# Dropping the value projection in the first stage: the sum over keys is taken over the normalised rows

## The chip, the cores and the metric

The kernel runs on one core of a Trainium2 chip. The metric is the device time of one execution in microseconds (us); lower is better. TensorE is written PE (its weight loads PEld), VectorE DVE, ScalarE ACT, GpSimd POOL, and the queue that issues most DMAs SP. "L672" is line 672 of the kernel before.

## The reference

Four layers follow each other on 16 x 256 tokens of width 128, each as `x = x + layer(layernorm(x))`: a linear attention with a small feed-forward network, a softmax attention with a mixture of experts, a second attention without softmax, and the softmax attention with the experts again. The change lies in the first layer only, whose attention is:

```python
Q = (x @ Wq + bq).reshape(N, L, H, Dh)       # N=16, L=256, H=16, Dh=8
K = (x @ Wk + bk).reshape(N, L, H, Dh)
V = (x @ Wv + bv).reshape(N, L, H, Dh)
Q = jax.nn.elu(Q) + 1.0
K = jax.nn.elu(K) + 1.0
KV = jnp.einsum('nshd,nshm->nhmd', K, V)
Ksum = K.sum(axis=1)
Z = 1.0 / (jnp.einsum('nlhd,nhd->nlh', Q, Ksum) + EPS_ATTN)
out = jnp.einsum('nlhd,nhmd,nlh->nlhm', Q, KV, Z)
```

## The kernel before

The first stage works on 16 pairs of 128-row tiles (one pair is one sequence of 256 tokens). It is a software pipeline written out by hand: on every engine `body(i, ...)` is emitted for i = 0, 1, 2, ..., and inside body i each block `if has(k)` does its step for pair p = i - k. An engine does its instructions in exactly this order, and where it waits for a semaphore (`wait_ge`, `after`), all that is queued behind waits too. Different engines use different k for the same pair, since each counts its own bodies.

TensorE's body i consists of, in this order (all matrix products are fp32; one such product shows as two matmul records):

- L577: the query product of pair i-1, 256 columns, into QM
- L589: transposes of z1 (second norm), pair i-7; L596: transposes of the attention rows, pair i-3; L606: attention product, pair i-2
- L619: second product of the feed-forward network, pair i-9
- L629: transposes of z0 (the normalised rows), pair i
- L636, L663: first product of the feed-forward network in halves, pairs i-8 and i-7; L647: output projection, pair i-4
- L656: the sum over keys of pair i-1: k_r (the keys after elu + 1) against v_r (the values with a column of ones), two products of 129 columns into KS
- L672: keys and values of pair i, two products of 256 columns into the bank KV

So the first bodies lack most steps: L647 comes in from i = 4, L663 and L589 from i = 7, L636 from i = 8, L619 from i = 9. In bodies 0 to 3 `spin` (L155) issues products of ones that nobody reads: three ahead of L629, one ahead of L672 and one ahead of L606. Body 5 also makes a weight product (L485), after L577.

ScalarE's body i: a relu (L690), z0 of pair i (L697, two instructions), exp of the keys of pair i-1 (L706), the copy of its values (L707), zt1 (L712), att_t (L717), exp of the queries (L722), a relu (L727), tmp (L735), the copy zt of the transposed z0 of pair i (L741, which adds the constant HAT), z1 (L749), and in bodies 4 and 5 a DMA issue (L564), in body 5 also a weight copy (L510).

VectorE makes k_r = max(min(exp, 1), rows) at L846 behind the statistics of a later pair (L537), and masks the sums from KS at L814 and L827. In its body 2 it also makes the small weight folds. GpSimd makes rstd and shift (L913, L915) for the three norms of an iteration in one go.

All weights of the stage carry a constant HAT trick: zt = z + HAT, and the bias row, scaled by ROW = 1/(128 HAT), is added to every row of the weights, so that the product brings the bias with it.

Of the kernel before, what the change touches and what calls it, by code (L numbers as in the profile page):

```python
# [84 lines left out]
def build(nc, A, out):  # L85

    ctx = ExitStack()
    with ctx:
# [41 lines left out]

        wa_qkv = sb("wa_qkv", [P, 3 * D])
        wa_o = sb("wa_o", [P, D])
# [36 lines left out]
        q_t = sb("q_t", [P, 3, 2 * P])  # L169
        v_r = sb("v_r", [P, 3, 2, P + 2])  # L170
        att_t = sb("att_t", [P, 3, 2 * P])
# [224 lines left out]
        hat_kept = sem("hat_kept")  # L396
        tokens_made = sem("tokens_made")
        k_cleared, p_cleared = sem("k_cleared"), sem("p_cleared")
        guarded = sem("guarded")

        @on("vector")
        def _(dve):
            nc.vector.memset(v_r[:, :, :, P:P + 1], 1.0).then_inc(rows_made, 1)
            dve.wait_ge(w_q_in, 16 * len(loads_q))

            nc.vector.tensor_scalar_add(row_a[0:1, 0:2 * D], row_a[0:1, 0:2 * D], 1.0).then_inc(rows_made, 1)

        def folds(dve):

# [12 lines left out]
            nc.vector.tensor_scalar_mul(b_low[:, :], b_low[:, :], 1.0 - 16 * B).then_inc(fold_step, 1)  # L422
            dve.wait_ge(fold_step, 4)
            nc.vector.tensor_scalar(token[:, :], token_f[:, :], b_low[:, 0:1], None, ALU.add).then_inc(tokens_made, 1)

# [3 lines left out]
        def hat(width, lhsT, rhs, bias, dst, **kw):  # L429
# [3 lines left out]

        hats_a = [hat(3 * D, centre[:, :], wa_raw[:, :], row_a[:, :], wa_qkv[:, :]),
                  hat(F, fold_a[:, :], wa1_raw[:, :], row_a2[:, :], wa1[:, :])]
# [98 lines left out]
        def bn(sources, slot, at, done):  # L534
# [5 lines left out]
        a_s = {n: sem("a_" + n) for n in (  # L540
            "n0", "n1", "n2", "step", "rstd", "shift", "z0", "z1", "z2", "turned", "turned1", "zt", "zt1", "kv_q", "read", "phi",
            "sums", "masked", "att", "inv", "att_r", "att_t", "wo", "xz", "r1", "hid", "relu", "w2", "y1", "r2", "xres", "xo")}
        a_stored = [sem(f"a_stored{n}") for n in range(3)]
# [24 lines left out]
        def _(pe):  # L568
# [3 lines left out]
            def body(i, s, has, lap):  # L572
# [36 lines left out]
                if has(9):  # L609
# [6 lines left out]
                    for t in range(2):  # L616
                        cut = slice(t * P, (t + 1) * P)
                        for m in range(FC):
                            last = nc.tensor.matmul(W2B[:, cut], hid[:, p % 2, m, cut], wa2[:, m, :], start=(m == 0),  # L619
                                                    stop=(m == FC - 1))  # L620
                    last.then_inc(g["w2"], 1)
                if has(0):
                    if i < 4:
# [25 lines left out]
                if has(1):  # L649
                    p = i - 1  # L650
                    pe.wait_ge(g["read"], first_of_two(p))
                    pe.wait_ge(g["phi"], first_of_two(p))
                    after(pe, g["masked"], p)
                    after(pe, g["r2"], i - 8)
                    for t in range(2):
                        last = nc.tensor.matmul(KS, k_r[:, p % 3, t, :], v_r[:, p % 3, t, 0:P + 1], start=(t == 0), stop=(t == 1))  # L656
                    last.then_inc(g["sums"], 1)
                if has(7):
# [7 lines left out]
                if has(0):  # L666
                    if i < 4:
                        spin(pe, bank[4], 1)
                    pe.wait_ge(g["zt"], i + 1)
                    after(pe, g["phi"], first_of_two(i - 1))  # L670
                    for t in range(2):
                        last = nc.tensor.matmul(KV[:, t * 256:(t + 1) * 256], zt[:, i % 3, 0, t * P:(t + 1) * P],  # L672
                                                wa_qkv[:, D:3 * D], start=True, stop=True)
                    last.then_inc(g["kv_q"], 1)
# [7 lines left out]
        def _(act):  # L682
            g = a_s

            def body(i, s, has, lap):
# [6 lines left out]
                if has(0):  # L692
                    act.wait_ge(g["shift"], i + 1)
                    after(act, g["turned"], i - 2)
                    after(act, g["xz"], i - 2)
                    for t in range(2):
# [3 lines left out]
                if has(1):  # L700
                    p = i - 1
                    act.wait_ge(g["kv_q"], first_of_two(p))
                    after(act, g["phi"], first_of_two(p - 3))
                    after(act, g["sums"], p - 2)
                    rows = KV[:, :].rearrange("p (t n) -> p t n", t=2)
                    nc.scalar.activation(exp_k[:, p % 3, :, :], rows[:, :, 0:P], ACT.Exp, bias=minus1[:, 0:1])  # L706
                    nc.scalar.activation(v_r[:, p % 3, :, 0:P], rows[:, :, P:2 * P], ACT.Copy).then_inc(g["read"], 1)  # L707
                if has(7):
# [29 lines left out]
                if has(0):  # L738
                    act.wait_ge(g["turned"], i + 1)
                    after(act, g["kv_q"], second_of_two(i - 3))  # L740
                    nc.scalar.activation(zt[:, i % 3, 0, :], TT[:, 0:256], ACT.Copy, bias=HAT).then_inc(g["zt"], 1)  # L741
                if has(6):
# [21 lines left out]
        def _(dve):  # L764
# [9 lines left out]
            def body(i, s, has, lap):  # L774
# [67 lines left out]
                if has(3):  # L842
                    p = i - 3
                    dve.wait_ge(g["read"], first_of_two(p))
                    rows = KV[:, :].rearrange("p (t n) -> p t n", t=2)
                    nc.vector.scalar_tensor_tensor(out=k_r[:, p % 3, :, :], in0=exp_k[:, p % 3, :, :], scalar=1.0,  # L846
                                                   in1=rows[:, :, 0:P], op0=ALU.min, op1=ALU.max).then_inc(g["phi"], 1)
                if has(7):
# [28 lines left out]
        def _(pool):  # L877
# [6 lines left out]
            def body(i, s, has, lap):  # L884
# [13 lines left out]
                if has(0) or has(7) or has(12):  # L898
# [15 lines left out]
                    pool.wait_ge(g["rstd"], i + 1)  # L914
                    nc.gpsimd.tensor_tensor(shift[:, c, w], nmean[:, c, w], rstd[:, c, w], ALU.mult).then_inc(g["shift"], 1)  # L915
                if has(12):
# [187 lines left out]
        def attention_block(n, src_dram, stored_before):  # L1104
# [217 lines left out]
            def _(dve):  # L1322
# [148 lines left out]
                else:  # L1471
                    dve.wait_ge(tokens_made, 1)
                nc.vector.memset(hot[:, 2, 1, :], 0.0).then_inc(cleared, 1)
# [230 lines left out]
        def block_b():  # L1704

            b_s = {k: sem("b_" + k) for k in (
                "stats0", "agg", "step", "rstd", "shift", "z", "turned", "zt", "gram", "gram_kept", "xw", "xw_kept", "fac", "fac_kept",
                "bo", "m", "m_kept",
                "out", "x3")}
# [119 lines left out]
            def _(dve):  # L1829
# [27 lines left out]
                dve.wait_ge(w_o_in, 16 * len(loads_o))  # L1857
                nc.vector.tensor_scalar_mul(bo[:, :], bo[:, :], ROW).then_inc(g["bo"], 1)
                dve.wait_ge(g["bo"], 1)
                pipeline(dve, PAIRS, DEPTH, 3, body, FIRST)  # L1860
# [84 lines left out]
```

## Time and profile before

| | before |
|---|---|
| timed runs | 684.54 us median of 3 (683.92 to 684.79) |
| span of the profiled execution | 684.5 us, 19055 instructions; no other time was recorded for it |
| TensorE busy (matmuls) | 637.8 us, 93% |
| TensorE weight loads | 545.5 us, 80% |
| VectorE | 483.9 us, 71% |
| ScalarE | 380.5 us, 56% |
| GpSimd | 398.7 us, 58% |
| the first stage | from the start to about 140 us |

Busy shares are averages over stages with different limits, so they only say where to look. For a stage one reads the waits of its engines and the chain of work that ended last. A record of a matmul is longer than the time it holds the array (records overlap, and their ends include the way through the array); the chain shows the time that each step really takes from the one before.

### The profile page before, as it was taken

The page shows a single profiled execution, that of the slowest core. Times are in us where ns is not written, and L with a number is a line of the kernel's source. Part 1 is how long each engine was busy: PE and PEld are TensorE (multiplying, and loading weights), DVE is VectorE, ACT ScalarE, POOL GpSimd, SP SyncE. Part 2 cuts the span into 40 slices and gives each one's busy share as a digit, 9 for nine tenths or more (in the row PEclk, how much of TensorE's full clock was granted, in tenths as well). Part 3 has the DMA queues.
Part 4 walks back from the last instruction along what each step waited for, and adds up shares of the span by engine and source line. Part 5 has one row for each costly group of instructions (what it writes and reads, how often), then busy time and mean ns, then how long its engine had stood idle before and what let it go on. Part 6 is the DMA issues. An engine that isn't in the chain of part 4 may idle for free.

```text
span 684.5 us, 19055 instructions
## 1 busy us (share of the span) xinstructions
PE 637.8 (93%) x5450; PEld 545.5 (80%) x5450; DVE 483.9 (71%) x2160; ACT 380.5 (56%) x974; POOL 398.7 (58%) x714
## 2 busy tenths in 40 slices
PE   8999999968999899999978999999699999999993
PEld 5899999836778679999975788787577877998993
DVE  2586777759999858888851333324899996887884
ACT  2587777648888435555523333330787864555550
POOL 5466668954688654767751121230548877467666
PEclk9999999989999989999999999999999999999997
DMA  4961001161122441232240000001312224332220
GB/s 126 325 234 30 17 25 33 36 203 27 44 74 88 168 134 54 85 85 78 59 133 7 24 17 24 15 23 49 109 31 73 78 92 119 83 85 76 81 69 21
DMA packets 57929, 53.63 MB, mean 78 GB/s; under 512 B 7707, under 2 KB 52164, under 8 KB 57532
## 3 DMA queue, kind: packets, MB, share of 16 engines
q1 hardware_dynamic: 51050, 36.19, 18.6%
q0 software_dynamic: 5568, 12.96, 5.5%
q10 hardware_dynamic: 1234, 3.55, 1.4%
q8 instruction: 37, 0.61, 0.4%
q14 instruction: 40, 0.33, 0.2%
HBM read 31.33 MB, written 19.83 MB: 75 GB/s over the span
## 4 chain that ended last, share of the span: by engine, by line
PE 44%; DVE 29%; issue 9%; POOL 8%; DVEq 4%; ACT 3%; DMA 2%; SPq 0%; POOLq 0%; ACTq 0%
PE wide L1794 4%; PE wide L1767 4%; DVE hid_f L1670 4%; PE wide L619 4%; PE bank L1780 4%; DVE stats L1666 3%; DVEq L1663 3%; POOL sorted_dram L1509 3%; POOL rstd L1495 3%; PE wide L155 2%; DVE late L1692 2%; PE bank L672 2%; PE wide L636 2%; PE wide L663 2%; PE wide L485 2%
## 5 line engine op out<-in xcount | busy, mean ns | idle before, releaser
L1608 PE MATMUL bank<-zt,late 128*128 128x128 f32 x624 | 92.8, 284 | 5.1 <-DVE hid_f L1670 4.7
L1608 PEld LDWEIGHTS bank<-zt,late 128*128 128x128 f32 x624 | 79.8, 191 | 11.9 <-DVE hid_f L1670 10.2
L1509 POOL DMA_INDIRECT sorted_dram<-rows_e,pos x64 | 66.0, 1031 | 26.1 <-issue 15.5
L1551 POOL TENSOR_TENSOR rstd<-var_e,half_neg 128x1 f32<-128x1 f32 x78 | 47.8, 613 | 43.3 <-DVE xout L1687 30.2
L1631 ACT ACTIVATE late<-we 128x512 f32 x80 | 50.5, 631 | 26.8 <-PE bank L1608 20.2
L1619 PE MATMUL wide<-late,hid_f 128*128 128x128 f32 x416 | 55.1, 275 | 1.1 <-DVE tmp L1675 1.1
L1619 PEld LDWEIGHTS wide<-late,hid_f 128*128 128x128 f32 x416 | 50.6, 192 | 1.4 <-issue 1.4
L1746 POOL TENSOR_TENSOR var_m<-mvs,eps 128x2 f32<-128x2 f32 x16 | 3.1, 194 | 79.5 <-DVE mvs L1847 79.5
L1851 DVE COPY late<-wide 128x1024 f32<-128x1024 f32 x16 | 19.6, 1225 | 39.0 <-PE wide L1794 39.0
L1558 POOL DMA_INDIRECT out<-xout,dest x39 | 40.6, 1041 | 10.4 <-issue 10.4
L1558 POOL DMA_INDIRECT x_dram<-xout,dest x39 | 40.5, 1039 | 8.1 <-issue 8.1
L1278 ACT ACTIVATE rows_e<-tmp,shift,rstd 128x128 f32<-128x128 f32 x64 | 28.1, 487 | 30.6 <-POOL shift L1497 30.6
L1638 ACT ACTIVATE zt<-bank 128x128 f32<-128x128 f32 x78 | 21.6, 277 | 41.7 <-PE bank L1598 39.9
L1495 POOL TENSOR_TENSOR rstd<-var_m,half_neg 128x2 f32<-128x2 f32 (+1 forms) x50 | 40.2, 804 | 4.3 <-DVE nmean L1380 0.9
L1492 POOL TENSOR_TENSOR var_m<-mvs,eps 128x2 f32<-128x2 f32 (+1 forms) x40 | 9.1, 228 | 56.6 <-DVE mvs L1442 26.5
L537 DVE BATCH_NORM_STATS2 stats<-xa 128x6 f32<-128x128 f32 (+1 forms) x128 | 29.4, 271 | 15.9 <-DMA xa<-x_dram 10.0
L1295 ACT ACTIVATE z<-xa,shift,rstd 128x128 f32<-128x128 f32 x64 | 28.0, 489 | 21.9 <-POOL shift L1497 21.9
L155 PE MATMUL wide<-ones 128*128 128x256 f32 x120 | 37.0, 447 | 3.2 <-DVE we L504 1.2
L1692 DVE COPY late<-we 128x640 f32 x78 | 38.2, 490 | 1.7 <-issue 1.7
L1670 DVE TENSOR_SCALAR hid_f<-bank 128x256 f32<-128x256 f32 x78 | 33.1, 425 | 6.7 <-issue 1.6
L1641 ACT ACTIVATE hid_f<-bank 128x256 f32<-128x256 f32 x78 | 29.9, 384 | 13.7 <-PE bank L1608 13.7
L1844 DVE TENSOR_TENSOR m_sb<-bank,bo 128x128 f32<-128x128 f32 x16 | 4.7, 292 | 39.2 <-PE bank L1780 39.2
(300 smaller groups left out, 1947.3 us busy)
## 6 DMA issues: line engine op xcount, KB each, us to landing
rows_e<-sorted_dram SPq DMA_DIRECT2D x78, 128.5 KB, 2.1
xa<-x_dram SPq DMA_DIRECT2D x9, 640.0 KB, 6.0
we<-L_ffn_W SPq DMA_DIRECT2D x16, 256.0 KB
x_dram<-xout SPq DMA_DIRECT2D x32, 128.0 KB, 1.8
early<-late SPq DMA_DIRECT2D x128, 32.0 KB
sorted_dram<-L_attn_a_x ACTq DMA_DIRECT2D x2, 1028.0 KB
rows_e<-L_ffn_b SPq DMA_DIRECT2D x1, 1024.0 KB
hid_f<-L_ffn_b ACTq DMA_DIRECT2D x1, 1024.0 KB
```

The lines of the kernel that those rows point to most:

```text
L155: nc.tensor.matmul(to[:, 0:2 * P], ones[:, :], ones2, start=True, stop=True)
L537: last = nc.vector.bn_stats(stats[:, slot, at + n, :], x)
L1495: nc.gpsimd.tensor_tensor(rstd[:, c, w], var_m[:, c, w], half_neg[:, w], ALU.pow).then_inc(g["rstd"], 1)
L1509: nc.gpsimd.indirect_dma_start(sorted_dram[n][:, :], bass.IndirectOffsetOnAxis(ap=pos[:, p % 3, t:t + 1], axis=0), pay[:, p % PAYS, t, :], ...
L1551: nc.gpsimd.tensor_tensor(rstd[:, s % 3, 0:1], var_e[:, s % 3, :], half_neg[:, 0:1], ALU.pow).then_inc(g["rstd"], 1)
L1558: nc.gpsimd.indirect_dma_start(target, bass.IndirectOffsetOnAxis(ap=dest[:, c, :], axis=0), xout[:, c, 0, :], None, bounds_check=T - 1, oo ...
L1608: last = nc.tensor.matmul(to[:, (m % 2) * P:(m % 2 + 1) * P], we_t[:, c1, m * P:(m + 1) * P], zt[:, c1, 0, 0:P], start=True, stop=True)
L1619: nc.tensor.matmul(VB[c2][:, 0:P], hid_e[:, c2, m, :], we_t[:, c2, F + m * P:F + (m + 1) * P], start=(m == 0), stop=False)
L1631: nc.scalar.activation(we_t[:, c, 0:F], we[:, bass.ds(e, 1), 0:F].rearrange("p a n -> p (a n)"), ACT.Copy).then_inc(g["w1"], 1)
L1641: nc.scalar.activation(hid_e[:, c1, 0:2, :], HA_[:, 0:256].rearrange("p (m t) -> p m t", m=2), ACT.Relu).then_inc(g["relu_a"], 1)
L1670: nc.vector.tensor_scalar_max(hid_e[:, c1, 2:4, :], HB_[:, 0:256].rearrange("p (m t) -> p m t", m=2), 0.0).then_inc(g["relu_b"], 1)
L1692: nc.vector.tensor_copy(we_t[:, c, F:], we[:, bass.ds(e, 1), F:].rearrange("p a n -> p (a n)"))\
```

## The change

The value projection goes. L672 makes only the keys (two products of 128 columns), and the sum over keys is taken over z0 itself, kz = z0^T k_r, in a new step on TensorE; ScalarE copies kz from PSUM to SBUF (new instruction), and one product of kz with the value weights (and a column ROW) gives the sums in KS. The values' copy L707 goes. The new step for pair i-1 stands ahead of L629 and, in bodies 0 to 3, ahead of the three spins; the product into KS stays where L656 was and now waits for the copy of kz, which ScalarE does right behind zt of pair i. Since z0 now takes part as rows with HAT in them, GpSimd adds HAT to shift in one more instruction, and zt is copied without it. The semaphore for two small VectorE steps is merged into another.

```diff
-        wa_qkv = sb("wa_qkv", [P, 3 * D])
+        wa_qkv = sb("wa_qkv", [P, 3 * D + 1])
...
-            nc.vector.memset(v_r[:, :, :, P:P + 1], 1.0).then_inc(rows_made, 1)
+            nc.vector.memset(wa_qkv[:, 3 * D:], ROW).then_inc(rows_made, 1)
```

TensorE, behind L619:

```diff
+                if has(1):
+                    p = i - 1
+                    pe.wait_ge(g["phi"], first_of_two(p))
+                    after(pe, g["kz_kept"], p)
+                    for t in range(2):
+                        last = nc.tensor.matmul(KV[:, 256:256 + P], z0[:, p % 3, t, :], k_r[:, p % 3, t, :], start=(t == 0),
+                                                stop=(t == 1))
+                    last.then_inc(g["kz"], 1)
                 if has(0):
                     if i < 4:
                         spin(pe, bank[4], 3)
...
                 if has(1):
                     p = i - 1
-                    pe.wait_ge(g["read"], first_of_two(p))
-                    pe.wait_ge(g["phi"], first_of_two(p))
+                    pe.wait_ge(g["kz_kept"], p + 1)
                     after(pe, g["masked"], p)
                     after(pe, g["r2"], i - 8)
-                    for t in range(2):
-                        last = nc.tensor.matmul(KS, k_r[:, p % 3, t, :], v_r[:, p % 3, t, 0:P + 1], start=(t == 0), stop=(t == 1))
-                    last.then_inc(g["sums"], 1)
+                    nc.tensor.matmul(KS, kz[:, p % 3, :], wa_qkv[:, 2 * D:], start=True, stop=True).then_inc(g["sums"], 1)
...
                     pe.wait_ge(g["zt"], i + 1)
                     after(pe, g["phi"], first_of_two(i - 1))
+                    after(pe, g["kz_kept"], i)
                     for t in range(2):
-                        last = nc.tensor.matmul(KV[:, t * 256:(t + 1) * 256], zt[:, i % 3, 0, t * P:(t + 1) * P],
-                                                wa_qkv[:, D:3 * D], start=True, stop=True)
+                        last = nc.tensor.matmul(KV[:, t * P:(t + 1) * P], zt[:, i % 3, 0, t * P:(t + 1) * P],
+                                                wa_qkv[:, D:2 * D], start=True, stop=True)
```

ScalarE:

```diff
                     act.wait_ge(g["kv_q"], first_of_two(p))
                     after(act, g["phi"], first_of_two(p - 3))
-                    after(act, g["sums"], p - 2)
-                    rows = KV[:, :].rearrange("p (t n) -> p t n", t=2)
-                    nc.scalar.activation(exp_k[:, p % 3, :, :], rows[:, :, 0:P], ACT.Exp, bias=minus1[:, 0:1])
-                    nc.scalar.activation(v_r[:, p % 3, :, 0:P], rows[:, :, P:2 * P], ACT.Copy).then_inc(g["read"], 1)
+                    nc.scalar.activation(exp_k[:, p % 3, :, :], KV[:, 0:256].rearrange("p (t n) -> p t n", t=2), ACT.Exp,
+                                         bias=minus1[:, 0:1]).then_inc(g["read"], 1)
...
-                    nc.scalar.activation(zt[:, i % 3, 0, :], TT[:, 0:256], ACT.Copy, bias=HAT).then_inc(g["zt"], 1)
+                    nc.scalar.activation(zt[:, i % 3, 0, :], TT[:, 0:256], ACT.Copy).then_inc(g["zt"], 1)
+                if has(1):
+                    p = i - 1
+                    act.wait_ge(g["kz"], p + 1)
+                    after(act, g["sums"], p - 2)
+                    nc.scalar.activation(kz[:, p % 3, :], KV[:, 256:256 + P], ACT.Copy).then_inc(g["kz_kept"], 1)
```

VectorE makes the same k_r from KV[:, 0:256] and waits ahead of it for the kz of three pairs before. GpSimd:

```diff
-                    nc.gpsimd.tensor_tensor(shift[:, c, w], nmean[:, c, w], rstd[:, c, w], ALU.mult).then_inc(g["shift"], 1)
+                    made = nc.gpsimd.tensor_tensor(shift[:, c, w], nmean[:, c, w], rstd[:, c, w], ALU.mult)
+                    if has(0):
+                        made.then_inc(g["centred"], 1)
+                        pool.wait_ge(g["centred"], i + 1)
+                        made = nc.gpsimd.tensor_tensor(shift[:, c, 0:2], shift[:, c, 0:2], hats[:, 0, 0:2], ALU.add)
+                    made.then_inc(g["shift"], 1)
```

## Rows read from the trace of the kernel before

**Rows 1.** Waits of PE from 10 to 131 us: who waited for whom, total us, times, longest.
```profile
PE wide L155 <- ACT wa_qkv L510: 0.6, 1, 0.6
```

**Rows 2.** Chain that ended last, two steady iterations: start us, us, engine, line, records.
```profile
61.03 0.45 PE wide L656 x4
...
62.34 0.86 PE bank L672 x4
...
64.57 1.78 PE wide L619 x16
66.35 0.22 PE bank L629 x2
66.57 0.87 PE wide L636 x4
67.44 0.45 PE wide L647 x4
67.88 0.45 PE wide L656 x4
```

**Rows 3.** The same chain in the first bodies and in body 5.
```profile
14.21 0.95 PE bank L672 x4
15.16 0.43 PE bank L577 x2
15.59 1.29 PE wide L155 x6
...
31.93 1.91 PE wide L485 x4
```

**Rows 4.** Timeline of all engines around pair 0: start us, us, engine, line, names.
```profile
15.20 0.47 ACT L706 ACTIVATE late<-bank,minus 128x256 f32<-128x256 f32 x1 [0.46 <-PE bank L672]
...
15.45 0.45 DVE L537 BATCH_NORM_STATS2 stats<-xa 128x6 f32<-128x128 f32 x2
15.57 0.38 ACT L707 ACTIVATE v_r<-bank 128x256 f32<-128x256 f32 x1
...
15.98 0.42 DVE L846 SCALAR_TENSOR_TENSOR early<-late,bank 128x256 f32<-128x256 f32 x1
...
16.81 0.19 POOL L915 TENSOR_TENSOR shift<-nmean,rstd 128x2 f32<-128x2 f32 x1
```

**Rows 5.** Timeline: the one place in the stage where L647 waits for ScalarE.
```profile
37.66 0.38 ACT L717 ACTIVATE att_t<-wide 128x256 f32<-128x256 f32 x1
...
38.09 0.71 PE L647 MATMUL wide<-wa_o,att_t 128*128 128x128 f32 x4
```

**Rows 6.** One line's instructions: ns min/median/max, first and last start, forms.
```profile
L1638 ACT ACTIVATE zt<-bank x78: 258/278/279, 253.7 to 667.9; 128x128 f32<-128x128 f32 x78
```

**Rows 7.** Timeline of ScalarE and its DMA issue (ACTq) in body 5.
```profile
34.96 0.38 ACT L741 ACTIVATE zt<-bank 128x256 f32<-128x256 f32 x1
...
35.24 0.59 ACT L510 ACTIVATE wa<-wide 128x512 f32<-128x512 f32 x1
...
35.41 0.71 ACTq L564 DMA_DIRECT2D sorted_dram<-L_attn_a_x  x1
...
36.25 0.88 ACT L697 ACTIVATE z<-xa,shift,rstd 128x128 f32<-128x128 f32 x2 [0.42 <-issue]
...
37.03 0.45 ACT L706 ACTIVATE late<-bank,minus 128x256 f32<-128x256 f32 x1
```

**Rows 8.** Timeline of PE in a later stage: a gap between products.
```profile
492.04 0.65 PE L1200 MATMUL bank<-early,late 128*32 128x128 f32 x16 [1.32 <-DVE early L1399]
```

**Rows 9.** Windows: PE, PEld, DVE, ACT, POOL busy us; granted clock; DMA share; GB/s.
```profile
362.00:364.00 2.00, 2.00 (x3) 0.97 (x4) 0.00 (x0) 0.67 (x2) 0.00 (x0) 0.51 0.00 0
...
490.00:492.00 2.00, 0.72 (x7) 0.48 (x5) 1.87 (x6) 1.65 (x7) 0.89 (x2) 1.00 0.03 8
```

**Rows 10.** The chain from the end of the first stage into the next.
```profile
133.42 3.61 PE bank L485 x12
...
138.62 3.38 DMA x_dram<-xout
```

More of the change, by code:

```diff
@@ L169, in build @@
         q_t = sb("q_t", [P, 3, 2 * P])
-        v_r = sb("v_r", [P, 3, 2, P + 2])
+        kz = sb("kz", [P, 3, P])
         att_t = sb("att_t", [P, 3, 2 * P])
@@ L396, in build @@
         hat_kept = sem("hat_kept")
-        tokens_made = sem("tokens_made")
         k_cleared, p_cleared = sem("k_cleared"), sem("p_cleared")
@@ L423, in folds @@
             dve.wait_ge(fold_step, 4)
-            nc.vector.tensor_scalar(token[:, :], token_f[:, :], b_low[:, 0:1], None, ALU.add).then_inc(tokens_made, 1)
+            nc.vector.tensor_scalar(token[:, :], token_f[:, :], b_low[:, 0:1], None, ALU.add).then_inc(fold_step, 1)
         HAT_BANK, HAT_BANK_B = (4, 5), (6, 7)
@@ L432, in hat @@
                         dst=dst, **kw)
-        hats_a = [hat(3 * D, centre[:, :], wa_raw[:, :], row_a[:, :], wa_qkv[:, :]),
+        hats_a = [hat(3 * D, centre[:, :], wa_raw[:, :], row_a[:, :], wa_qkv[:, 0:3 * D]),
                   hat(F, fold_a[:, :], wa1_raw[:, :], row_a2[:, :], wa1[:, :])]
@@ L540, in build @@
         a_s = {n: sem("a_" + n) for n in (
-            "n0", "n1", "n2", "step", "rstd", "shift", "z0", "z1", "z2", "turned", "turned1", "zt", "zt1", "kv_q", "read", "phi",
-            "sums", "masked", "att", "inv", "att_r", "att_t", "wo", "xz", "r1", "hid", "relu", "w2", "y1", "r2", "xres", "xo")}
+            "n0", "n1", "n2", "step", "rstd", "centred", "shift", "z0", "z1", "z2", "turned", "turned1", "zt", "zt1", "kv_q", "read", "phi",
+            "kz", "kz_kept", "sums", "masked", "att", "inv", "att_r", "att_t", "wo", "xz", "r1", "hid", "relu", "w2", "y1", "r2", "xres", "xo")}
         a_stored = [sem(f"a_stored{n}") for n in range(3)]
@@ L694, in body @@
                     after(act, g["turned"], i - 2)
+                    after(act, g["kz"], i - 2)
                     after(act, g["xz"], i - 2)
@@ L844, in body @@
                     dve.wait_ge(g["read"], first_of_two(p))
-                    rows = KV[:, :].rearrange("p (t n) -> p t n", t=2)
+                    after(dve, g["kz"], p - 2)
                     nc.vector.scalar_tensor_tensor(out=k_r[:, p % 3, :, :], in0=exp_k[:, p % 3, :, :], scalar=1.0,
-                                                   in1=rows[:, :, 0:P], op0=ALU.min, op1=ALU.max).then_inc(g["phi"], 1)
+                                                   in1=KV[:, 0:256].rearrange("p (t n) -> p t n", t=2), op0=ALU.min,
+                                                   op1=ALU.max).then_inc(g["phi"], 1)
                 if has(7):
@@ L1471, in _ @@
                 else:
-                    dve.wait_ge(tokens_made, 1)
+                    dve.wait_ge(fold_step, 5)
                 nc.vector.memset(hot[:, 2, 1, :], 0.0).then_inc(cleared, 1)
@@ L1707, in block_b @@
                 "stats0", "agg", "step", "rstd", "shift", "z", "turned", "zt", "gram", "gram_kept", "xw", "xw_kept", "fac", "fac_kept",
-                "bo", "m", "m_kept",
+                "m", "m_kept",
                 "out", "x3")}
@@ L1857, in _ @@
                 dve.wait_ge(w_o_in, 16 * len(loads_o))
-                nc.vector.tensor_scalar_mul(bo[:, :], bo[:, :], ROW).then_inc(g["bo"], 1)
-                dve.wait_ge(g["bo"], 1)
+                nc.vector.tensor_scalar_mul(bo[:, :], bo[:, :], ROW).then_inc(fold_step, 1)
+                dve.wait_ge(fold_step, 6)
                 pipeline(dve, PAIRS, DEPTH, 3, body, FIRST)
```

## The prediction

> **What bounds the kernel now.** The change touches the first stage alone, so the shares of the whole page only say that TensorE comes first. I read the waits of TensorE in the stage first: from 10 to 131 us there is one wait of its matmuls in the list, 0.6 us behind a weight copy [rows 1]. Next the chain of work that ended last: through the whole stage it is made of TensorE's steps alone, one starting where the last ends. A steady iteration (from i = 9, when all steps are there) takes 67.88 - 61.03 = 6.85 us, all of it products [rows 2]. In the first bodies the chain is gapless too, but there it runs through the spins [rows 3]. The reader should see two things. TensorE's columns are the price of a steady iteration; and in bodies 0 to 8 the spins and the order of the steps just cover the way through ScalarE and VectorE, so a step moved forward there may lose its cover. The end of the stage hangs on TensorE as well: its last products, then x1 goes out and comes back by DMA, with no slack in the chain [rows 10]. So what the stage gains or loses reaches the end in full.
>
> **TensorE's own work.** L672 falls from 256 columns to 128 in each of two products: 0.87 us (62.34 to its end) to the 0.45 us that four records of 129 columns take at L656 [rows 2]; gain 0.42 x 16 pairs = 6.7 us. The new kz step is two products of 128 columns, 0.45 us, as much as L656 took, and L656 becomes one product, half of 0.45, 0.22 us. So 0.22 x 16 = 3.5 us are added. Net: 3.2 us less, 0.20 us in each full iteration.
>
> **Instructions that cost nothing by themselves.** ScalarE loses a copy of 0.38 us [rows 4] and gains one of 128x128, for which L1638 has 0.28 us [rows 6]. GpSimd gets one more addition of about 0.19 us [rows 4] and a semaphore. shift is made an iteration ahead of the z0 and z1 that use it, so some 4 us of slack hide it; without that cover it would delay z0 by 0.25 us per pair. The merged semaphores and the memset are nothing: same place, same count of waits. No DMA moves.
>
> **The price of a wait on TensorE.** What is queued behind a waiting product is everything. The row for it: att_t ends at 37.66 + 0.38 = 38.04 and the four records that waited for it end at 38.09 + 0.71 = 38.80 [rows 5]. So from the producer's end to the end of two 128-column products it is 0.76 us, where they hold the array 0.45 in the stream; for one product I take 0.76 - 0.22 = 0.54. An engine that waits for TensorE starts 0.04 us after a step's end (15.16, then 15.20) [rows 3, 4].
>
> **Wait 1, kz for k_r.** kz(i-1) now stands ahead of the spins and of L629. The way to it from the end of L672, which I call t: exp 0.04 to 0.51, then k_r 0.42 more, so ready at t + 0.97 or when VectorE gets to it.
> - Body 1: L672 ends 0.42 earlier, at 14.74, L577 at 15.17. exp ends at about 15.25 and no longer has the copy behind it, but VectorE is busy with folds and statistics until 15.45 + 0.45 = 15.90, so k_r moves only from 15.98 to about 15.88 and ends at 16.30 [rows 3, 4]. kz ends at 16.30 + 0.76 = 17.06 and not at 15.17 + 0.45 = 15.62: wait 1.44 us. Before, three spins of 1.29 us in all stood in this place [rows 3]. They now come after it.
> - Bodies 2 and 3: a spin and L606 lie between, 0.43 + 0.43 + 0.49 from t; k_r is in time.
> - Body 4: no spin, 1.14 us from t, and k_r about t + 1.07 (VectorE's statistics first) with the start-up: 0.2 us.
> - Body 5: the weight product, 1.91 us, hides it [rows 3].
> - Body 6: ScalarE is held by its own queue. From zt at 34.96 to the exp at 37.03 it is 2.07 us of weight copy, DMA issue and z0 [rows 7]; with the kz copy in it about 2.3 us, while L672 will end 1.6 us after L629. So exp is 0.7 late, k_r ends 3.2 us after L629 and kz about 4.0, against 3.1 if it had no wait: 0.9 us. The wait of L647 in the same body, 0.25 us, goes under it [rows 5].
> - Body 7: z1 and z0, two pairs of 0.88 us [rows 7], now follow the later zt and kz copy; exp is about 0.5 late, wait 0.5 us.
> - From body 8 the new distance from t grows to 1.36 us, from body 9 (L619) to 3.1 us [rows 2]: no wait.
> Sum 1.44 + 0.2 + 0.9 + 0.5 - 0.25 = 2.8 us.
>
> **Wait 2, KS for the copy of kz.** The copy stands behind zt, and zt needs L629 of the same body. From the end of L629: 0.04, then 0.28 from the start of zt to the next instruction's start (34.96, 35.24) [rows 7], then 0.28 for the copy: ready at 0.60; KS ends 0.54 later, at 1.14. In bodies 1 to 3 KS follows L629 at once and would end at 0.22, so 0.92 is waited, three times 2.8 us. In bodies 4 to 7 L647 of 0.45 lies between: 0.47, four times 1.9 us. From body 8 L636 comes in too (0.87 + 0.45 = 1.32 us) [rows 2], and the copy is in time with about 0.5 us to spare. The mask on VectorE comes as much later, but what waits for it, L606, is in the next body. Nor does ScalarE hold anything longer: its next instructions, z1 and z0, shift by the copy's 0.28 and have over 2 us in the steady part.
>
> **Sum.** 2.8 + (2.8 + 1.9) - 3.2 = +4.3 us by the parts. Followed from body to body, with the rounding and the small delays of the rows (L672 of body 0 had 0.95) it comes to +3.9. I take +4.1: 684.5 + 4.1 = 688.6 us. The median of the runs shown is 684.54, the profiled span 684.5, so nothing has to be converted. Bounds of this case: if ScalarE's queue holds nothing in bodies 6 and 7, it is 1.2 less; if VectorE comes later there or the start-up after a wait is 0.1 dearer each of ten times, it is 1.0 more. Its own range is 687.2 to 689.8.
>
> **The rivals.**
> - *The columns win* (other side). The waits are hidden: k_r is ready in time in body 1 and the kz copy reaches KS in bodies 1 to 7. Then 3.2 us are gained: 681.3 us. For it: exp no longer shares its turn with the copy, and from i = 9 on I find slack of 0.5 and 1.6 us, where the gain is sure. Against it: it decides at a sum of waits under 3.2 us, and the three of body 1 to 3 behind L629 alone, which nothing in the order covers, are 2.8, the one of body 1 for VectorE 1.4. Chance 0.05.
> - *Half of the waits*: the chain cuts them to 2 to 4.5 us, because the spins were longer than needed and the engines catch up. 683.5 to 685.8 us, mostly no change. Chance 0.09. Against it: spins are counted, not timed, so none gets shorter when a wait comes.
> - *The clock falls.* The new idle gaps come right after TensorE has come up to speed. In the trace a gap of 1.32 us in a stretch with 0.72 busy of 2 us keeps the granted clock at 1.00 (2.4 GHz), while 362 to 364 us, in another stage, shows 0.51 (1.2 GHz) [rows 8, 9]. If it fell once, 2 to 3 us of products would take double: +1 to 1.7 us, twice +3: 689.7 to 692. The Trainium skill speaks for this rival: in "TensorE: Matmul & The Clock Gate", section "A second HAM failure mode: psum-queue depth-cycling", frequent short idles between groups of matmuls make the clock swing between its two levels. By that rule this rival's time would hold; the trace at 490 to 492 us does not agree (clock 1.00). Chance 0.08.
> - *The steady part waits too*: if ScalarE is over 0.5 us later with the kz copy than I find, KS waits in each of nine iterations, and 0.2 to 0.4 each gives 690.5 to 692. Chance 0.04.
>
> **How the numbers follow.** The forecast has 0.74. A fifth of a per cent is about what a measurement of this kernel can tell from no change, so the bounds are 683.2 and 685.9. Slower: 0.74 + 0.08 + 0.04 and a little of the second rival, 0.87; within: 0.07; faster: 0.06. The range 685.6 to 690.6 takes in the forecast's own range, the upper edge of the half-way rival and the cheaper part of the two dear ones.
>
> **What would show it.** In the profile after: new waits of TensorE's weight loads, kz for VectorE's k_r about 1.4 us in body 1 (near 15 to 16.5 us), again near 42 and 46 us; KS for ScalarE's kz copy, near 0.9 three times and near 0.5 four times; the three spins behind kz; a steady period of 6.65 us without waits; granted clock 1.00; the stage's end about 4 us later and the later stages unchanged. The prediction is wrong if the waits of the first eight bodies come to under 4 us or if a wait shows in the steady iterations.

## The result, and the profile after

The changed kernel takes 689.81 us (median of 6, 687.95 to 695.8), the kernel before 683.88 (683.36 to 684.79): ratio 1.0097, interval 1.0059 to 1.0135, slower by 5.9 us. The forecast was 688.6 us, range 685.6 to 690.6. The profiled execution is the longest of the six: 695.8 us, span 694.0, 9.5 us over the span of before. So two questions are left: are the parts those of the sum, and what are the 1.2 us (median) to 7.2 us (longest) on top of it? The 5.9 us are a difference of medians; by the ratio it is 6.6.

Line numbers of after: kz is L626, KS L661, keys L677, queries L576, transposes of z0 L636, attention product L605, feed-forward L618, L643, L667, output projection L654; k_r L855, exp of the keys L710, zt L745, copy of kz L750.

The waits of TensorE from 10 to 140 us, by its matmuls (total, times, longest); where before there was one [rows 1]:

```profile
PE bank L626 <- DVE early L855: 4.7, 3, 4.2
PE wide L661 <- ACT kz L750: 2.7, 7, 0.6
```

These are the two waits of the forecast: KS seven times, bodies 1 to 7, and kz for k_r. But the longest is 4.2 us, not 1.4. (The list counts idle time of the matmuls only. A product that had to wait also has a longer record: kz 0.71 us and not 0.45, KS 0.49 and not 0.22. So a wait costs about 0.27 us more than the list has.) The chain that ended last, from body 1 on (start, us); kz, L626, opens a body, the keys, L677, close it:

```profile
16.25 1.22 PE bank L626 x4
17.47 2.56 PE wide L155 x6
20.03 0.44 PE bank L636 x2
...
20.49 0.38 ACT zt L745
20.88 0.18 ACT kz L750
...
21.10 0.80 PE wide L661 x2
...
27.30 0.23 PE bank L636 x2
...
27.84 0.28 ACT kz L750
...
28.16 0.49 PE wide L661 x2
28.65 0.43 PE wide L155 x2
29.09 0.44 PE bank L677 x4
...
34.63 0.44 PE bank L677 x4
...
61.10 0.45 PE bank L626 x4
...
67.76 0.45 PE bank L626 x4
```

From the end of the transposes (27.53) the kz copy starts 0.31 us later (0.32 forecast) and KS ends at 28.65, 1.12 us (1.14 forecast). Body 3, from L677 to L677, takes 34.63 - 29.09 = 5.54 us. Before, it was 27.43 - 22.59 = 4.84:

```profile
22.59 0.86 PE bank L672 x4
...
27.43 0.86 PE bank L672 x4
```

That is 0.70 more; 0.92 of waiting less 0.20 for the columns had been forecast, 0.72. The steady iteration is 61.10 to 67.76, 6.66 us (6.65 forecast, 6.85 before [rows 2]), with no wait. What is not in the forecast is the start of this list: six spins take 2.56 us, where [rows 3] has 1.29. The timeline around it:

```profile
11.45 0.60 PE L576 MATMUL bank<-zt,wa_qkv 128*128 128x256 f32 x2
...
13.55 0.48 DVE L536 BATCH_NORM_STATS2 stats<-xa 128x6 f32<-128x128 f32 x2 [4.47 <-DMA xa<-L_attn_a_x]
...
15.11 0.24 DVE L423 TENSOR_SCALAR token<-token_f,b_low 128x32 uint32<-128x32 f32 x1
...
15.79 0.41 DVE L855 SCALAR_TENSOR_TENSOR early<-late,bank 128x256 f32<-128x256 f32 x1
...
16.25 1.22 PE L626 MATMUL bank<-early,z 128*128 128x128 f32 x4 [4.20 <-DVE early L855]
```

and the windows (PE, PEld, DVE, ACT, POOL busy us; granted clock; DMA share; GB/s):

```profile
13.00:14.00 1.00, 0.00 (x0) 0.00 (x0) 0.45 (x3) 0.00 (x0) 0.00 (x0) 1.00 1.17 289
14.00:15.00 1.00, 0.00 (x0) 0.00 (x0) 0.93 (x7) 0.00 (x0) 0.00 (x0) 0.73 0.39 65
15.00:16.00 1.00, 0.00 (x0) 0.00 (x0) 0.96 (x7) 0.00 (x0) 0.34 (x2) 0.50 0.38 58
...
24.00:26.00 2.00, 2.00 (x13) 1.79 (x12) 0.82 (x3) 0.59 (x2) 0.00 (x0) 0.82 0.94 336
```

In this execution TensorE had full speed early and was done with the queries of pair 0 at 12.05 us, where in the profile of before it was 15.59 [rows 3]. VectorE, however, starts the statistics of pair 2 when its tile lands, 13.55 us, then makes the folds, and k_r(0) comes at 15.79 as it did before (15.98 [rows 4]). TensorE stands for 4.2 us; the granted clock goes to 0.50 (1.2 GHz) and is back within the window of 24 to 26 us. The first stage hands over where its last rows go out by DMA (the first line with x_dram), at 146.30, before at 138.62 [rows 10]:

```profile
146.30 3.41 DMA x_dram<-xout
...
484.06 1.82 DMA x_dram<-xout
```

That is 7.7 of the 9.5 us. The rest falls behind it: from the first to the second line with x_dram it is 337.8 us against 335.5 before. It isn't the change's: the same stretch is 334.7 in the second profile of this same kernel, and 338.2 in one of the kernel before with other loads (136.80 to 474.95).

### The profile page after: what moved, and what is told of

Read it like the earlier page. It is cut to its first block, busy times and chain, and to the rows that moved or that the text cites. A ratio compares the mean times of both kernels' runs of the same rounds, so it can differ in the third digit from the quotient of the medians.

```text
span 694.0 us, 19180 instructions
## 1 busy us (share of the span) xinstructions
PE 639.7 (92%) x5482; PEld 547.8 (79%) x5482; DVE 481.9 (69%) x2160; ACT 380.7 (55%) x974; POOL 402.4 (58%) x730
## 4 chain that ended last, share of the span: by engine, by line
PE 43%; DVE 28%; issue 10%; POOL 8%; DVEq 3%; DMA 3%; ACT 3%; ACTq 1%; POOLq 0%; SPq 0%
PE wide L1809 4%; PE wide L1782 4%; PE wide L618 4%; PE bank L1795 4%; DVE hid_f L1685 4%; POOL sorted_dram L1524 3%; DVE stats L1681 3%; DVEq L1678 3%; POOL rstd L1510 3%; PE wide L155 2%; PE bank L1623 2%; DVE late L1707 2%; DVE stats L536 2%; PE wide L643 2%; PE wide L667 2%
## 5 line engine op out<-in xcount | busy, mean ns | idle before, releaser
L536 DVE BATCH_NORM_STATS2 stats<-xa 128x6 f32<-128x128 f32 (+1 forms) x128 | 29.4, 271 | 18.6 <-DMA xa<-x_dram 12.7
L1782 PE MATMUL wide<-wk,gram 128*128 128x512 f32 x64 | 32.1, 626 | 0.4 <-ACT gram L1834 0.4
```

The costliest lines, as they stand in the source:

```text
L536: last = nc.vector.bn_stats(stats[:, slot, at + n, :], x)
L1782: last = nc.tensor.matmul(XW[:, 512 * k:512 * (k + 1)], gram[:, c2, :], wk[:, 512 * k:512 * (k + 1)], start=True, stop=True)
```

## The experiments

All were timed in turns with the kernel before on the same chip, and a ratio is to that. Three chips were used: one for after_again, kr0_early, kr0_copy and keys_only, one for fill_gap, the two with other loads and kr0_copy_guards, one for the rest. Medians are compared on one chip only, from chip to chip the ratios. Most kernels build on one another: kr0_copy on kr0_early, kr0_copy_folds on kr0_copy, order_all on kr0_copy_folds, order_fewer_spins on order_all.

### The changed kernel again

> The changed kernel once more, unchanged, to see how much of its time varies. My theory: the steady parts are fixed (period 6.65 us, kz copy waits of about 0.5 us), and what varies is the wait of kz(0) for k_r(0) in body 1, which VectorE makes only behind tile data that land near 13.5 us, and with it the clock: where the wait is over 3 us the granted clock falls to half and the stage loses some 3 to 4 us more. Expected: 688 us in executions without a fall, up to 696 with it, median near 689.5. The rival, that the steady part costs more than I found, expects all executions at one time and new waits from body 9 on.

Measured: 692.04 us (688.51 to 696.54, 6 executions), ratio 1.0100, interval 1.0059 to 1.0142. The median is 2.5 us over what I expected, and outside the range of the prediction. Its profile has the same picture: kz(0) waits 3.0 us for k_r and the clock falls; the KS waits are the same, and there are none from body 9 on, so the rival is out. The timeline:

```profile
16.70 1.22 PE L626 MATMUL bank<-early,z 128*128 128x128 f32 x4 [3.00 <-DVE early L855]
```

and a window, its columns as above:

```profile
20.00:25.00 5.00, 4.36 (x15) 3.40 (x14) 1.23 (x5) 1.84 (x6) 0.00 (x0) 0.50 1.04 354
```

The twelve executions of the two sets run from 687.95 to 696.54. Their lower end is near the forecast. The mean granted clock of an execution goes with its time: 0.985 in the fastest of each set, 0.968 and 0.966 in the two slowest. Some 10 us at 0.50 in bodies 1 and 2 make about 0.007 of such a mean (my estimate: half of 10 in 690), so part of this difference lies in other places. No profile was taken of an execution of this lower end, so that there is no fall in body 1 in them is not shown.

### k_r of pair 0 ahead of the data wait

```diff
+                if i == 2:
+                    keys_phi(0)
                 if has(0):
                     for n, (lo, hi) in enumerate(X_PARTS):
                         if lo <= 2 * i < hi:
                             dve.wait_ge(x_back[n], 16)
...
-                if has(3):
...
+                if has(3) and i > 3:
+                    keys_phi(i - 3)
```

> Edit on the changed kernel: VectorE makes k_r of pair 0 ahead of the statistics of pair 2 and so ahead of the wait for the third part of x, and not behind the folds and the statistics of pair 3. My theory (kz(0) is coupled to the arrival of x and the folds, and the long gap drops the clock): the wait of kz(0) falls to about 1 us, the clock stays whole in the first stage, 687.3 us and a spread of under 1.5 us, instead of 689.8 with a spread of 8. If the gap is not what drops the clock, the spread stays near 8 us and the median falls by 0.5 to 1 at most.

Measured: 685.40 us (683.76 to 688.73), ratio 1.0009, interval 0.9988 to 1.0030: 6.6 us under the changed kernel on the same chip, more than expected. keys_phi(p) is the k_r step of before as a function; the added call makes k_r of pair 0. The two longest waits of kz are now 0.66 and 1.11 us, the granted clock is 1.00 from 10 to 30 us, and the stage hands over at 140.47 and not at 146.98, 6.5 us earlier. So this one wait and what it does to the clock are worth about as much as the change costs in all over the kernel before; what is left, the KS waits above all, is about what the columns give. Eleven of the twelve lie within 683.8 to 686.6: narrower than the 8 us of after_again, but not the 1.5 us that I expected. The 1.11 us are kz(1), which now waits in its turn. Its chain runs from the third part of x through the folds and statistics, GpSimd's shift with the added addition (0.20 us at 17.50), z0 of pair 2 and the exp behind it.

```profile
12.71 0.71 PE L626 MATMUL bank<-early,z 128*128 128x128 f32 x4 [0.66 <-DVE early L786]
19.48 0.71 PE L626 MATMUL bank<-early,z 128*128 128x128 f32 x4 [1.11 <-DVE early L786]
```

### The gap filled, the wait kept

```diff
+                if i == 1:
+                    spin(pe, bank[4], 9)
                 if has(1):
                     p = i - 1
                     pe.wait_ge(g["phi"], first_of_two(p))
...
-                    if i < 4:
+                    if i < 4 and i != 1:
                         spin(pe, bank[4], 3)
```

> Edit on the changed kernel: in body 1 TensorE issues nine spins (3.9 us at 2.4 GHz) ahead of kz(0), and none behind it, where there were three; every wait and every other engine stays as it is. This takes the gap away and not what it waits for. My theory (the gap is what drops the clock, and the clock makes up the difference between 688 and 692): kz(0) still starts when k_r is ready at about 16.3 us, but the clock stays at 1.00 from 10 to 25 us, kz to the end of body 2 runs at full speed, 688 us and the stage's fall gone. If the clock falls for another reason (the start of the kernel, which windows it meets), the spins change nothing: 692 us and 0.50 in the windows from 15 to 25 us.

Measured: 688.17 us (685.27 to 692.11), ratio 1.0051, interval 1.0031 to 1.0072, against 1.0100 for the changed kernel. TensorE does six spins more than the changed kernel (2.6 us of useless work), no wait is taken out of the code, and it is 3.4 us faster by the ratios. The windows:

```profile
10.00:15.00 5.00, 5.00 (x22) 4.11 (x21) 1.17 (x7) 2.06 (x5) 0.65 (x3) 0.73 0.92 243
15.00:20.00 5.00, 4.36 (x26) 3.80 (x25) 2.74 (x16) 1.32 (x5) 3.47 (x11) 1.00 0.69 184
20.00:25.00 5.00, 4.36 (x27) 3.78 (x26) 2.06 (x11) 2.21 (x6) 2.11 (x6) 1.00 1.01 346
```

The clock is whole from 13 us on, where it was 0.50 to 0.54 from 15 to 20 us in both profiles of the changed kernel. I had expected it whole from 10 us: the 0.73 in the first row is an earlier fall, 0.50 from 10 to 12 us, ahead of the nine spins. This separates the two: the gap's own length is one part, the clock that it drops is the other.

The edit does one thing more. It takes the three spins behind kz(0) away, and this kz starts later, at 17.28. The transposes that follow end at 17.96 us, in after at 20.47 (20.03 + 0.44). 2.00 of these 2.51 us are the clock (the records of kz, spins and transposes twice as long, less those at full speed), 0.5 is the order of the spins. From there to the handover, at 142.05, it is 124.1 us against 125.8. So in the profiles 4.25 us are gained up to the handover, 3.8 of them by the clock; the two intervals of the timed sets overlap, and their 3.4 us can't tell 3 from 4. All in all 0.51% over before is 3.5 us, where the forecast, with a whole clock and the spins behind kz, was 4.1.

### The copy of kz ahead of zt

```diff
+                if has(1):
+                    p = i - 1
+                    act.wait_ge(g["kz"], p + 1)
+                    after(act, g["sums"], p - 2)
+                    nc.scalar.activation(kz[:, p % 3, :], KV[:, 256:256 + P], ACT.Copy).then_inc(g["kz_kept"], 1)
                 if has(0):
                     act.wait_ge(g["turned"], i + 1)
...
```

> As kr0_early, and ScalarE copies kz ahead of zt, not behind it. My theory (KS waits for a copy that stands behind zt): kz is ready 0.22 us ahead of the transposes, so the copy ends 0.36 us after kz; the wait of KS falls from 0.92 to about 0.4 in bodies 1 to 3 and from 0.47 to nearly 0 in bodies 4 to 7, together 3.3 us under kr0_early: 684.0 us. zt comes 0.1 to 0.2 us later, covered by KS. If the waits of KS come from something else (the bank that kz and the keys share, or the semaphores), it is as kr0_early, 687.3.

Measured: 683.25 us (681.47 to 688.33), ratio 0.9978, interval 0.9957 to 0.9999; 2.2 us under kr0_early. From here on the changed kernel is 0.2% under the kernel before, just clear of the noise; whether it is also under a kernel before with the same repairs comes below. The waits of KS are gone altogether (first kernel: kr0_early; second: kr0_copy):

```profile
PE wide L661 <- ACT kz L750: 2.7, 7, 0.6
PE bank L626 <- DVE early L786: 2.3, 4, 1.1
```

```profile
PE bank L626 <- DVE early L786: 2.5, 4, 1.1
PE bank L576 <- DVE q_t L795: 1.1, 1, 1.1
```

I had expected 0.4 us each to be left in bodies 1 to 3. That overlooked the spins: in those bodies they stand between kz and the transposes, so the copy has 1.3 us more. The gain is 2.2 and not 3.3 us because what the KS wait of body 1 gives back stops at body 2. There TensorE, earlier now, waits 1.1 us for q_t of VectorE and then 1.1 us for k_r of pair 1, whose chain starts with the data of pair 2. kz(1) starts at 20.17 us in this profile and at 19.48 in that of kr0_early, where the data landed 0.7 us sooner (13.97 and not 14.67). From kz(1) to the handover it is 117.8 us against 121.0, 3.2 less.

### Keys alone: what the columns are worth

```diff
-                        last = nc.tensor.matmul(KV[:, t * 256:(t + 1) * 256], zt[:, i % 3, 0, t * P:(t + 1) * P],
-                                                wa_qkv[:, D:3 * D], start=True, stop=True)
+                        last = nc.tensor.matmul(KV[:, t * P:(t + 1) * P], zt[:, i % 3, 0, t * P:(t + 1) * P],
+                                                wa_qkv[:, D:2 * D], start=True, stop=True)
...
```

> Edit on the kernel before: L672 makes only the keys, 128 columns instead of 256, and ScalarE's copy takes the keys' columns in the place of the values, so the value projection is left out and nothing is put in its place. My theory (columns on TensorE are the price, 0.42 us per pair): 683.9 - 6.7 = 677.2 us, steady period 6.42 us. If TensorE is held by weight loads or by another engine in the stage, the gain is under 3 us.

This kernel leaves out the value projection, so its output is wrong; it only serves to price the columns.

Measured: 679.80 us (677.58 to 683.03), ratio 0.9927, interval 0.9900 to 0.9954: 4.8 us less than before by the medians, 3 to 7 by the interval, which holds the 6.7. The steady iteration is 6.43 us (6.42 expected):

```profile
64.38 0.45 PE wide L656 x4
...
70.81 0.45 PE wide L656 x4
```

So columns are the price there. In the profile the handover is 5.6 us earlier than before (133.04), and what is short of 6.7 goes at two places. At the start KS of pair 0 now waits 1.7 us for k_r: the same tie to the arrival of x, which the kernel before comes near. And from L672 of body 4 to L672 of body 7 it takes 12.40 us (29.30 to 41.70) where before it was 12.89 (30.64 to 43.53): 0.49 less, where three times 0.42 is due. There the chain runs through ScalarE's queue (exp, weight copy, DMA issue and z0, 32.49 to 39.36). So bodies 5 to 7 have next to no slack in the kernel before either.

### The loads of x

The second DMA of x brings pairs 1 and 2: `X_PARTS = ((0, 2), (2, 6), (6, 16), (16, 32))`, once on kr0_copy and once on the kernel before.

> As kr0_copy, and the second DMA of x brings pairs 1 and 2 (256 KB), the third starts at pair 3. Theory: in kr0_copy the chain of bodies 1 and 2 runs through the third part of x, which lands at 14.7 us, VectorE's folds, GpSimd's shift, z0 of pair 2 and exp of pair 1, which stands behind z0 in ScalarE's queue. With pair 2 there 3 us or more earlier, kz(1) is ready 2 to 3 us sooner: 681 us. If the folds' own data (which come with other loads) hold VectorE as long, it gains under 0.5: 683.

> The same edit of the loads on the kernel before. There the sums of pair 0 stand behind three spins, and its chain in the profile runs through TensorE alone, so I expect nothing: 684.6 us, within 0.5. If the kernel before is held by the same data in the executions where TensorE is at full speed early, it gains 1 us or more.

Measured on one chip: kr0_copy_xearly 683.33 us, ratio 0.9979 (0.9962 to 0.9996), as kr0_copy had; before_xearly 683.01 us, ratio 0.9978 (0.9960 to 0.9996). So the earlier data alone give the repaired kernel nothing, and I was wrong on both: nothing where I expected 2 us, 0.2% where I expected nothing. With the same loads, the repaired kernel and the kernel before take the same time. The profile of kr0_copy_xearly shows one reason. VectorE stands idle for 5.8 us ahead of k_r of pair 0, which now is first in its queue, and the folds and the statistics of pair 2 start only behind it, however early the data are:

```profile
15.28 0.42 DVE L786 SCALAR_TENSOR_TENSOR early<-late,bank 128x256 f32<-128x256 f32 x1 [5.80 <-ACT late L710]
```

This is an execution in which TensorE is slow at the start. In one with full speed early, exp and k_r of pair 0 come sooner; what the loads do there is not shown. The profiled executions differ in how early TensorE has full speed (kr0_copy_xearly makes its first product in 3.21 us, before_xearly in 1.73), so they don't explain the second.

### The folds out of the way

```diff
-                if i == 2:
+                if i == 3:
                     folds(dve)
```

> As kr0_copy, with VectorE's weight folds in its body 3 and not in body 2. In the trace of kr0_copy the wait of kz in body 2 (1.1 us) ends a chain that runs from the third part of x through the folds (15.1 to 16.4 us), the statistics, GpSimd's shift, z0 of pair 2 and exp of pair 1 behind it. Theory: the folds are on it, so 1.1 to 1.3 us come off: 682.1 us. If the data alone set it (the earlier loads had changed nothing, though), 683.3.

> The kernel before with the same two repairs that can be made there: folds in body 3 and pair 2 in the second DMA of x. A fair base for the repaired kernels. Expected 683.0 us, as with the loads alone, since in its traces TensorE waits for nothing in the stage but for the sums of pair 0 in executions that start at full speed; 0.5 us less at most.

Measured on one chip: kr0_copy_folds 681.66 us (679.68 to 686.11), ratio 0.9960, interval 0.9938 to 0.9983. By the ratios that is 1.2 us under kr0_copy, as expected, though the intervals overlap. The wait of 1.1 us of kz in body 2 is gone from its trace, and one of 0.9 us for q_t stays. before_folds_xearly: 683.43 us (681.30 to 686.13), ratio 0.9989 (0.9973 to 1.0005). Together with before_xearly it leaves open whether these repairs give the kernel before 0.1 or 0.2%, or nothing. It is the fair base for the repaired kernels: kr0_copy_folds is 1.8 us under it by the medians, and the two intervals overlap. So the repaired change is likely to be faster than the kernel before with like repairs, by some 0.3%, but that is hardly clear of the noise.

### Whose queue holds k_r in body 6

Two edits on one wait. The first moves ScalarE's DMA issues from bodies 4 and 5 to 9 and 10 (on kr0_copy); the second makes VectorE's k_r in its bodies 4 to 8 ahead of the statistics (on kr0_copy_folds, with the loads).

> As kr0_copy, with ScalarE's two DMA issues moved from bodies 4 and 5 to 9 and 10. The prediction put the wait of kz(5) on ScalarE's queue: then exp comes 0.7 us earlier and the wait of kz in body 6 goes, 0.5 to 0.9 us. The trace of after has exp done 0.4 us before VectorE gets to k_r, so VectorE's queue behind KS should hold it: then exp comes earlier and the wait in body 6 stays within 0.1 us.

> As kr0_copy_folds, with pair 2 in the second DMA of x, and in VectorE's bodies 4 to 8 k_r made ahead of the statistics of r1 and x. Theory: the two waits of kz in bodies 6 and 7, 0.6 us each, are VectorE's queue (statistics of 0.9 us ahead of k_r), so they fall to 0.1 or nothing, and the data of pair 2 are off the way: 680.5 us, which is the kernel before less about 4, near its 3.2 us of spared products. If ScalarE's queue held the exps as the prediction had it, the waits stay and the time is 681.7 or more.

The timeline around kz(5) in the three, exp (L710), statistics (L536) and k_r (L786) after the copy of kz(4) (L746). kr0_copy:

```profile
35.13 0.28 ACT L746 ACTIVATE kz<-bank 128x128 f32<-128x128 f32 x1 [0.19 <-PE bank L626]
...
37.11 0.45 ACT L710 ACTIVATE late<-bank,minus 128x256 f32<-128x256 f32 x1
37.27 0.47 DVE L536 BATCH_NORM_STATS2 stats<-xa 128x6 f32<-128x128 f32 x2
37.66 0.40 DVE L786 SCALAR_TENSOR_TENSOR early<-late,bank 128x256 f32<-128x256 f32 x1
```

kr0_copy_guards, a single execution (683.16 us):

```profile
34.32 0.28 ACT L746 ACTIVATE kz<-bank 128x128 f32<-128x128 f32 x1 [0.19 <-PE bank L626]
...
36.06 0.47 ACT L710 ACTIVATE late<-bank,minus 128x256 f32<-128x256 f32 x1
36.46 0.47 DVE L536 BATCH_NORM_STATS2 stats<-xa 128x6 f32<-128x128 f32 x2
36.84 0.41 DVE L786 SCALAR_TENSOR_TENSOR early<-late,bank 128x256 f32<-128x256 f32 x1
```

order_all (682.71 us, 678.67 to 684.46, ratio 0.9958, 0.9941 to 0.9976; expected 680.5, so a miss, and no gain over the 0.9960 of kr0_copy_folds):

```profile
33.65 0.28 ACT L746 ACTIVATE kz<-bank 128x128 f32<-128x128 f32 x1 [0.19 <-PE bank L626]
33.96 0.71 ACTq L563 DMA_DIRECT2D sorted_dram<-L_attn_a_x  x1
35.64 0.45 ACT L710 ACTIVATE late<-bank,minus 128x256 f32<-128x256 f32 x1
36.12 0.42 DVE L786 SCALAR_TENSOR_TENSOR early<-late,bank 128x256 f32<-128x256 f32 x1 [0.64 <-ACT late L710]
```

From the copy to k_r it is 2.53, 2.52 and 2.47 us. Free ScalarE's queue and exp is 0.24 us earlier, but k_r stays behind the statistics; take the statistics away and k_r waits for an exp that the DMA issue and the weight copy hold. In kr0_copy the two queues end within 0.1 us of each other (exp 37.56, k_r starts 37.66), so neither edit alone gives anything. The prediction named ScalarE only, the expectations of these two runs VectorE; both are there. I didn't run both edits together, and order_all didn't touch the wait of kz(6): its k_r is in VectorE's body 9. Both waits, 0.3 us each and 0.26 for the longer record behind, stay in all three.

### Fewer spins

Without the three spins in bodies 2 and 3, on order_all.

> As order_all, without the three spins ahead of the transposes in bodies 2 and 3 (1.29 us each). Theory: spins are counted and not timed; where nothing waits they cost their own time: 2 x 1.29 = 2.6 us less, 677.9 us, unless z0 of the next pair or the kz copy becomes the wait: then 1 us less. If the spins are needed for the clock, the granted clock falls between 20 and 30 us and the time rises.

Measured: 680.42 us (677.75 to 683.44), ratio 0.9944, interval 0.9928 to 0.9961; 2.3 us under order_all on the same chip, 2.6 expected; the intervals overlap. (The 677.9 expected started from order_all's expected 680.5.) The clock stays at 1.00 from 5 to 30 us. Body 2 by the chain, L677 to L677:

```profile
15.96 0.53 PE bank L677 x4
...
18.33 0.29 ACT kz L746
...
18.66 0.49 PE wide L661 x2
...
19.58 0.45 PE bank L677 x4
```

3.62 us; 4.5 in order_all (17.08 to 21.58). The 1.29 us of spins come off and 0.4 of it goes back into a KS wait, which the spins had covered. This is the fastest complete kernel of the study, 0.56% under before. How much of that is the change's is open: the same three spins stand in the chain of the kernel before too (1.29 us at 20.20 and at 25.03), and that kernel without them was not run.

## Why the prediction was right, and where not

**Sign and mechanism were right.** TensorE bounds the stage; the columns give 0.2 us in a steady iteration (6.66 after 6.85); kz loses its cover in body 1, KS seven times. kr0_early and kr0_copy undo the two waits one by one and give 6.6 and 2.2 us, after which the kernel is 0.2% under before. That the number came so near is in part luck: up to the handover the profile has 7.7 us where 4.1 were forecast, with a clock fall that was given a chance of 0.08, and the second set's median, 692.04, lies outside the range.

**Wait 2** (2.8 + 1.9 us) was right in size: 1.12 us from the transposes to the end of KS against 1.14 (0.90 of it more than without a wait in bodies 1 to 3, 0.45 in 4 to 7, 4.5 us in all), and body 3 dearer by 0.70.

**Wait 1 in bodies 6 and 7** was right in size (0.3 and 0.2 us idle, and records of 0.71 us for 0.45: 0.57 and 0.48 for 0.9 and 0.5. Body 6 is 0.69 us longer than before by the chain, where the terms said 0.9 - 0.25 + 0.47 - 0.20 = 0.92) and half right in cause: VectorE's queue is as late as ScalarE's.

**Wait 1 in body 1 was mis-sized**: 1.44 us in the sum, 4.2 and 3.0 in the two profiles. The step took TensorE's side from the one trace of before, where the first product and six spins ran at half speed (3.2 and 2.9 us) until 13.1. In after TensorE reached this point 3.5 us earlier, 0.4 of it by the narrower keys. k_r's side did not move, since it hangs on a DMA and VectorE's order: 15.79 for 15.88 forecast. A wait for something with a fixed time grows by all that the waiting engine gains before it, so the earlier start gained nothing here; the step should have had this as its upper bound.

**"The clock falls" was given 0.08 and took place in both profiles.** Its price, 1 to 1.7 us for one fall, was too small, and its working doesn't hold: 2 to 3 us of products at half speed cost 2 to 3 us more, not 1 to 1.7, and no row said how long the clock stays down. From 16.25 to 25.1 us each step at half speed, kz 1.22 for 0.71, six spins 2.56 for 1.29, the transposes 0.44 for 0.22, KS 0.80 for 0.49, a spin, the keys and the queries 0.42 more each and 0.19 for a part of the next spin, makes 3.8 us. fill_gap confirms about that much (1.0100 to 1.0051, with the 0.5 us named there). The argument against it had a gap of 1.3 us as its row; the gaps that came were 4.2 and 3.0.

**One "nothing" was not quite nothing.** The mask on VectorE comes later, and in the body without transposes and keys the attention product L605 waits for it, 0.35 us longer by the chain (111.07, 0.76 us long and not 0.49). GpSimd's extra addition and the moved copies cost nothing that shows in after: no wait in the steady bodies. At the start that holds only while kz(0) is later; in kr0_early the addition is in the chain of kz(1).

The sum by the parts for the profile, against the 7.7 us at the handover. kz costs 5.5 us: 4.7 idle, and 0.26 for the record behind each of the three waits. Body 4 adds 0.15 (its kz 0.59 for 0.44), KS 4.5, the clock 3.8, L605 0.35. Off go 0.25 for the wait of L647 that went under, 3.2 for the columns and 3.1 for the earlier arrival of TensorE at body 1 (3.5 without the 0.4 that the narrower keys give). That makes 7.7.

## What to carry to other kernels

When a step is moved ahead in a hand-ordered pipeline, cost it in the first bodies, where steps are missing and filler work was its cover; a gain per steady iteration is quickly spent there (here 3.2 us in all against waits of 7.5 in the forecast and about 14, with the clock, in the profile). Ask of each new wait whether its other side is fixed in time (a DMA, a queue behind one): then anything won before it only lengthens the gap, and a long gap can cost a second time through the clock (here 3.8 us behind a gap of 4.2). And where two queues feed one operation and end together, moving one shows nothing; that moving both would, was not run here. And compare a repaired kernel with a base that has the same repairs: kr0_copy_xearly was 0.2% under the kernel before, and not under the kernel before with the same loads.

## What the runs showed of the hardware

- The start differs between executions whose order on TensorE is the same: the first weight product takes 3.21 us in one (6.43 to 9.64, before) and 1.73 in another (6.21 to 7.94, before_xearly), with the granted clock at 1.00 up to 8 us in both, and in before all the way. The matmul records show it, the clock column doesn't.
- A wait of 3.0 and one of 4.2 us with TensorE idle brought the granted clock to 0.50, and it was back only within 24 to 26 us, some 8 to 9 us after work had begun again. The Trainium skill, "TensorE: Matmul & The Clock Gate", section "HAM oscillation — how this bites in real kernels", has long idle gaps as what drops it, and these two traces agree; gaps of 0.7 to 1.1 us (kr0_early, kr0_copy) and of 1.7 (keys_only) left it at 1.00.
- Not every fall had such a gap. In six of the fourteen profiles (after_again, fill_gap, keys_only, before_xearly, kr0_copy_guards, order_all) the granted clock was 0.50 from about 9 to 12 us, with TensorE idle for at most 0.9 us at a time from 6 us on; in the other eight, with idle times of the same size or longer (1.3 us in after), it stayed at 1.00 there. What made the difference is open. In after_again (columns as above) it was back at 1.00 from 12 us on, ahead of the wait of 3.0 us:

```profile
9.00:10.00 1.00, 1.00 (x3) 0.82 (x4) 0.23 (x2) 0.73 (x2) 0.61 (x3) 0.50 0.23 61
```

- Otherwise equal stretches, from the handover near 140 us to the one near 475, took 332.9 to 338.2 us over all kernels. These 5 us are more than most of the differences here: a single profiled execution can't carry them.
